# Two-block network on one core: the attention probabilities' 16-bit halves turned by a DMA transpose, one per head, instead of by TensorE

## The reference

```python
G = NUM_HEADS // NUM_KV_HEADS
q = jnp.einsum('bth,oh->bto', x, Wq).reshape(B, T, NUM_HEADS, HEAD_DIM).transpose(0, 2, 1, 3)
k = jnp.einsum('bth,oh->bto', x, Wk).reshape(B, T, NUM_KV_HEADS, HEAD_DIM).transpose(0, 2, 1, 3)
v = jnp.einsum('bth,oh->bto', x, Wv).reshape(B, T, NUM_KV_HEADS, HEAD_DIM).transpose(0, 2, 1, 3)
q = q * cos + _rotate_half(q) * sin
k = k * cos + _rotate_half(k) * sin
qg = q.reshape(B, NUM_KV_HEADS, G, T, HEAD_DIM)
scores = jnp.einsum('bkgtd,bksd->bkgts', qg, k) * scale
scores = jnp.where(causal, scores, -jnp.inf)
attn = jax.nn.softmax(scores, axis=-1)
out = jnp.einsum('bkgts,bksd->bkgtd', attn, v)
return jnp.einsum('bto,ho->bth', out, Wo)
```

## Time and profile before

| | |
|---|---|
| median of 3 runs | 2485.41 us |
| the profiled execution | 2484.75 us, span 2482.8 us |
| busy share of the span | PE 96%, PEld 55%, DVE 72%, ACT 64%, POOL 50% |
| mean granted TensorE clock | 0.986 of full speed |
| DMA, mean share of 16 engines | 27% for the kernel's own queue |
| the attention | about 1597 to 2345 us from the start |
| one pass over eight heads in it | 88.20 us |

### The profile page before, as it was taken

How to read it: one execution, slowest core, us unless ns; L and a number is a source line. 1 busy time by engine, 2 the same in 40 slices (tenths; PEclk the granted TensorE clock), 3 DMA queues, 4 the chain that set the end, 5 groups by cost and what they waited for, 6 DMA issues and landing times. The chain is left out here.

```text
span 2482.8 us, 48888 instructions
## 1 busy us (share of the span) xinstructions
PE 2378.8 (96%) x15424; PEld 1368.9 (55%) x15624; DVE 1787.9 (72%) x3234; ACT 1591.7 (64%) x3327; POOL 1232.0 (50%) x986
## 2 busy tenths in 40 slices
PE   6999999999999999999999998879999999999797
PEld 3555555555555555555555555445555555555443
DVE  6777777777777777777777776577777777788522
ACT  7676776776776776776776775265665656656422
POOL 4455555555555556556556459344434343454223
PEclk8999999999999999999999999999999999999999
DMA  7343343343343343343343341230110110100000
GB/s 248 108 129 111 108 128 111 108 133 105 113 132 107 110 133 109 106 137 109 102 140 109 119 151 56 103 124 1 43 43 1 44 44 1 43 18 1 1 0 34
DMA packets 113827, 218.79 MB, mean 88 GB/s; under 512 B 9632, under 2 KB 43040, under 8 KB 111360
## 3 DMA queue, kind: packets, MB, share of 16 engines
q1 hardware_dynamic: 113536, 215.28, 26.6%
HBM read 212.10 MB, written 3.15 MB: 87 GB/s over the span
## 5 line engine op out<-in xcount | busy, mean ns | idle before, releaser
L256 DVE SCALAR_TENSOR_TENSOR xc<-bank,taps,xc 128x511 f32<-128x511 f32 (+2 forms) x384 | 284.7, 742 | 44.6 <-ACT xc L243 27.4
L984 ACT ACTIVATE E<-wq,cst 128x128 f32<-128x128 f32 x1024 | 311.8, 390 | 2.2 <-PEq L298 2.2
L1268 POOL TENSOR_TENSOR xw<-xt,wdec 128x384 f32<-128x384 f32 x128 | 106.4, 832 | 327.3 <-DVE xt L1119 163.7
L1277 POOL TENSOR_TENSOR acc<-acc,sq 128x512 f32<-128x512 f32 x112 | 172.0, 1536 | 186.8 <-ACT sq L996 186.8
L1911 POOL TENSOR_TENSOR qT<-qT,qrot 128x512 f32<-128x512 f32 x64 | 81.3, 1270 | 368.6 <-DVE qrot L1801 368.6
L1161 DVE SCALAR_TENSOR_TENSOR u<-xc,D,bank 128x512 f32<-128x512 f32 x128 | 95.6, 747 | 210.3 <-PE bank L813 198.8
L1100 DVE TENSOR_TENSOR E<-E,cbm 128x1024 f32<-128x1024 f32 x128 | 242.9, 1898 | 0.8
L61 PE MATMUL bank<-xhi,wx 128*128 128x512 f16 x640 | 242.5, 379 | 0.0
L60 PE MATMUL bank<-xlo,wx 128*128 128x512 f16 x640 | 242.5, 379 | 0.0
L59 PE MATMUL bank<-xhi,wx 128*128 128x512 f16 x640 | 242.5, 379 | 0.0
L1263 POOL TENSOR_TENSOR ecs<-ecs,xcC 128x768 f32<-128x768 f32 x128 | 234.1, 1829 | 0.4 <-POOLq L298 0.4
(11 more groups left out here) (237 smaller groups left out, 6299.4 us busy)
## 6 DMA issues: line engine op xcount, KB each, us to landing
wq<-cs_rows SPq DMA_DIRECT2D x128, 512.0 KB, 4.1
ecs<-ecs_rows SPq DMA_DIRECT2D x128, 384.0 KB, 3.6
wx<-in_w_xbc SPq DMA_DIRECT2D x80, 256.0 KB, 2.7
wz<-in_w_z SPq DMA_DIRECT2D x64, 256.0 KB, 2.7
wo<-in_w_o SPq DMA_DIRECT2D x64, 256.0 KB, 4.0
wq<-in_wq SPq DMA_DIRECT2D x8, 1024.0 KB, 5.7
awo<-in_wo SPq DMA_DIRECT2D x8, 1024.0 KB, 5.0
wkv<-in_wkv SPq DMA_DIRECT2D x8, 512.0 KB, 3.7
```

Of the source, the lines that this page charges most:

```text
L256: self.nc.vector.scalar_tensor_tensor(out=dst[:, d:T], in0=self.k.bank[bank][:, 0:T - d], scalar=self.taps[:, bass.ds(g, 1), b, j, 3 - d:4 ...
L984: ins = nc.scalar.activation(E[t.i % 4][:, h, c], sc.csr[t.i % 2][:, h, c * P:(c + 1) * P], ACT.Relu, scale=-1.0, bias=head(sc.cst, t, c, h))
L1277: nc.gpsimd.tensor_tensor(acc[t.b][:], acc[t.b][:], sq[:], ALU.add).then_inc(acc_done, 1)
```

## The change

- The probabilities are split into halves before they are turned. ACT writes the scaled leading half (`leading_p`) and DVE the rest (`rest_of_p`, now four scalar_tensor_tensor, each reading the fp32 probabilities in SBUF, a scalar per partition, and the leading half in SBUF) into one buffer `phalves` of 20 blocks, ordered so that row block i's rest blocks lie at 5i to 6i and its leading blocks at i + 1, i + 6, and so on.
- SP issues one DMA transpose a head (`turn`) from `phalves` into one of two buffers `pturned`, 20 blocks of 128 x 128 of 16 bits (640 KB). It waits for `rest_of_p` of that head and for `attend` of two heads before. `leading_p` of the next head waits for the transpose to land, `attend` waits for it too, and `exps` waits for `rest_of_p` of the head before, since `probs` is one buffer now.
- PE's ten transposes a head, ACT's three copies and their banks are gone. The projections use four banks in turn (0, 1, 5, 6) in place of two.
- ACT takes the value's leading half from the PSUM bank, and DVE its rest half from the bank (after ACT), where DVE had copied and POOL had subtracted.
- The SwiGLU weights are loaded one piece a head, behind that head's transpose, and the per-column scale `dscale` at the start of the SwiGLU.

```diff
@@ in attention: buffers
-        pr = [sb(f"probs{i}", [P, 1280]) for i in range(2)]
+        pr = sb("probs", [P, 1280])
-        pthi, ptlo = sb("pthi", [P, 1280], F16), sb("ptlo", [P, 1280], F16)
+        ph = sb("phalves", [P, P_BLOCKS * P], F16)
+        pt = [sb(f"pturned{i}", [P, P_BLOCKS, P], F16) for i in range(2)]
@@ SP
+                def turn(n, h):
+                    sp.wait_ge(p_lo, n + 1)
+                    sp.sem_inc(step, 1)
+                    if not (isinstance(n, int) and n < 2):
+                        sp.wait_ge(pv_ready, n - 1)
+                        sp.sem_inc(step, 1)
+                    sp.dma_start_transpose(out=pt[h % 2][:], in_=ph[:]).then_inc(pt_in, 16)
...
+                            if later(g, b, h, 1):
+                                turn(n + 1, h + 1)
+                            if isinstance(g, int) and g < 2:
+                                load_swiglu(k, io, sp, n)
@@ PE
-                            turn(n, h, [0], None)
-                            turn(n, h, [1], None)
...
-                                pe.wait_ge(proj_free, ahead - 1)
+                                ring_free(pe, ahead)
...
-                            turn(n, h, [2, 3], 3 * n + 1)
...
+                    pe.wait_ge(pt_in, 16 * n + 16)
                     for j in range(CH):
...
+                                     (pt[h % 2][:, 6 * j + 1:5 * j + 5], pt[h % 2][:, 6 * j:16 + j:5]), j == 0, j == CH - 1)
@@ ACT
+                def leading_p(n, h):
                     act.wait_ge(exp_done, n + 1)
                     act.wait_ge(rsum_done, n + 1)
+
+                    wait(act, pt_in, 16 * n)
                     for i in range(CH):
+                        nc.scalar.activation(leading_blocks(i), probs(i), ACT.Copy,
+                                             scale=rsum[h % 2][:, i:i + 1]).then_inc(p_hi, 1)
...
-                def leading_v(u, b):
-                    act.wait_ge(v_ok, u + 1)
-                    nc.scalar.copy(vhi[b][:], v[:]).then_inc(kv_hi, 1)
+                def leading_v(u, b, ahead, bank):
+                    act.wait_ge(proj_ready, ahead + 1)
+                    nc.scalar.copy(vhi[b][:], bank[:, :].rearrange("p (t d) -> p t d", d=P)).then_inc(kv_hi, 1)
@@ DVE
-                        nc.vector.tensor_copy(v[:], k.bank[bank][:, :].rearrange("p (t d) -> p t d", d=P)).then_inc(v_ok, 1)
-                        dve.wait_ge(v_ok, u + 1)
+                        dve.wait_ge(kv_hi, 2 * u + 2)
+                        nc.vector.tensor_tensor(vlo[b][:], bank[:, :].rearrange("p (t d) -> p t d", d=P), vhi[b][:],
+                                                ALU.subtract).then_inc(v_lo, 1)
...
-                def rest_of_p(n, u):
-                    bank, at, size = EVAC[u]
-                    dve.wait_ge(pt_hi, 3 * n + u + 1)
-                    nc.vector.tensor_tensor(ptlo[:, at:at + size], k.bank[bank][:, 0:size], pthi[:, at:at + size],
-                                            ALU.subtract).then_inc(pt_lo, 1)
+                def rest_of_p(n, h):
+                    for i in range(CH):
+                        dve.wait_ge(p_hi, 4 * n + i + 1)
+                        out = ph[:, 5 * i * P:(6 * i + 1) * P].rearrange("p (b t) -> p b t", t=P)
+                        ins = nc.vector.scalar_tensor_tensor(out=out, in0=probs(i), scalar=rsum[h % 2][:, i:i + 1],
+                                                             in1=leading_blocks(i), op0=ALU.mult, op1=ALU.subtract)
+                    ins.then_inc(p_lo, 1)
@@ POOL
-                                rest_of_v(g * NB + b + 1, 1 - b)
```

More of the change, by code:

```diff
@@ L1572, in ring, with ring_free @@
                 ahead -= QH
-            return (g * NB + b) * 10 + (PRO + ahead), (PRO + ahead) % 2
+            return (g * NB + b) * 10 + (PRO + ahead), k.bank[RING[(b * 10 + PRO + ahead) % 4]]
+        def ring_free(pe, ahead):
+            wait(pe, proj_free, ahead - 3)
         LAST_OUT = (NG * NB - 1) * 10 + (PRO - QH) + 5
@@ L1662, in output @@
                         w = wo[s][:, h]
-                        mm = product(nc, k.bank[bank][:, :], (ohi[b][:, h, x], olo[b][:, h, x]), (lead(w), rest(w)),
+                        mm = product(nc, bank[:, :], (ohi[b][:, h, x], olo[b][:, h, x]), (lead(w), rest(w)),
                                      h == 0, h == QH - 1)
@@ L1767, in body @@
                             n = item(g, b, h)
-                            for u, (bank, at, size) in enumerate(EVAC):
-                                if u == 2 and later(g, b, h, 1):
-                                    normalise(n + 1, h + 1)
-                                act.wait_ge(pt_ready, 3 * n + u + 1)
-                                nc.scalar.copy(pthi[:, at:at + size], k.bank[bank][:, 0:size]).then_inc(pt_hi, 1)
+                            if later(g, b, h, 1):
+                                leading_p(n + 1, h + 1)
                             if later(g, b, h, 3):
@@ L1871, in body @@
                                 scales(n + 1, h + 1)
-                            for u in range(2):
-                                rest_of_p(n, u)
                             for i, (kind, what) in enumerate(uses):
@@ L1878, in body @@
                                     serve(kind, ahead, bank, n + 3, 0, what[1], what[2])
-                                elif kind != "o":
+                            if later(g, b, h, 1):
+                                rest_of_p(n + 1, h + 1)
+                            for i, (kind, what) in enumerate(uses):
+                                ahead, bank = ring(g, b, h, i)
+                                if kind in "kv":
                                     serve(kind, ahead, bank, 0, g * NB + b + 1, what[1], 0)
-                            rest_of_p(n, 2)
                             if later(g, b, h, 2):
@@ L2220, in program @@
             k.di = k.sb("di", [P, IT, HS], I32, early)
-            k.gs, k.us, k.dscale = (k.sb(n, [P, m], F32, early) for n, m in (("gs", IT), ("us", IT), ("dscale", HS)))
+            k.gs, k.us = (k.sb(n, [P, IT], F32, early) for n in ("gs", "us"))
             k.ffn_in = k.sem("ffn_in")
```

159 lines of the change are left out of this document (75 added, 84 removed).

## The result

The changed kernel takes 2637.67 us in the median of 4 runs (2633.57 to 2639.35), where the kernel before, run beside it, took 2486.03 (2484.25 to 2489.18). The ratio is 1.0606, with a 95% interval of 1.0588 to 1.0624: 6% slower, 152 us. The forecast was 2645.

A forecast was written before the change was run, and what follows sets the result against it. PE was taken to bound the kernel at 9.75 us a head, the DVE-ACT loop close under it at 9.12. POOL's holds on the new rests add 160 us to 2484.75: 2645 us, range 2540 to 2770 (forecast's own 2600 to 2710).

The forecast's parts named there:

- The loop without the collision: DVE-ACT loop of a plain head, from scales to scales, with the new rests but no POOL hold: 9.48 us.
- No collision: Rival: the new rests don't meet POOL at all, so the kernel gets faster, 2476 us; chance 0.07.
- The collision: DVE's rests wait for POOL instructions reading SBUF: 1.05 behind the addition, 1.65 the split, 0.9 the query's rest.
- The estimate with a full block: The same three POOL holds on DVE's rests if the port lock is exclusive: 4.2 us, a head 13.7.
- The sum: Whole kernel: seven groups +145, last group some +15, first four heads +3, less 3 for overlapping edges: +160 us.
- The h = 1 head: Head also projecting key and value: the value's rest waits for ACT's leading half, 16.0 us against 14.85.
- the estimate of 26 us: Transpose of 20 blocks in a row at the skill's 1.31 us a block; a head of 29, 3600 us in all.
- Up to 8 us it costs nothing: DMA transpose, taken as 4.0 us, is hidden up to 8 us; above that 1 us a head for each.
- PE's clock: Idle PE may run at a lower clock: nothing taken, at most 1 us a head (+64) for the range.
- two signs: Expected in the changed profile: PE waits 4 us a head ahead of scores; its busy share falls to two thirds.
- DVE keeps its turn: Rival: the four rests run through once started, only POOL's addition is paid, +59, 2544 us; chance 0.13.
- a slow transpose: Rival: from 8 us on the DMA transpose sets the pace; at 14.8 us, 2906 us in all; chance 0.19.

The follow-up runs named there:

- e_psum: Changed kernel with projections on two banks again and the four rests reading their first input from PSUM bank 5, not the SBUF probabilities: 2466.98 us, ratio 0.9921.
- e_hold_v_n: Changed kernel with POOL's rotation addition waiting for the four rests, ACT taking the value's leading half first, and negated maxima on ACT: 2462.15 us, ratio 0.9894.
- e_vfirst: Changed kernel with ACT taking the value's leading half before the key's, and the two waits that count them exchanged: 2603.02 us, ratio 1.0459.
- e_split: Changed kernel with POOL's weight split of a head put ahead of the rotation sum instead of behind it: 2587.33 us, ratio 1.0404.
- e_copy: Changed kernel with each head's DMA transpose replaced by a plain DMA copy of the same 640 KB: 2631.04 us, ratio 1.0577.
- e_hold_v_n_twice: e_hold_v_n with each head's transpose done twice, the second after the first has landed: 2628.8 us, ratio 1.0572.

## Why the prediction was right, step by step

- **The loop without the collision** was 9.48 us; e_psum, which has no collision, shows 9.32 (1868.20 to 1877.52, starts of `scales`). The terms: `scales` to rotation 0.29 and not 0.47 (1819.52 to 1819.81; the 0.47 of the earlier trace rows runs to the old rests, not to a rotation), rotation 2.28, rests 1.94 against 1.9, mask to next `scales` 4.82 from the rows (2.61 + 2.21) and 4.82 measured (1827.47 to 1832.29). "No collision" was to give 2476, and e_psum gives 2467.
- **The collision** was the step that decided, and it holds term by term. First rest, behind the addition: 1.34 against 0.35 alone, +0.99 (charged 1.05). Second, behind the split: 2.11 against 0.48, +1.63 (1.65). Third, behind the query's rest: 1.51 against 0.65, +0.86 (0.9). Together 3.5 against 3.6. The durations alone are from the groups by shape of e_hold_v_n (busy us, mean ns):

```profile
L1855 DVE SCALAR_TENSOR_TENSOR phalves<-probs,rsum,phalves 128x384 f16<-128x384 f32 x57 | 37.0, 648 | 0.0
...
L1855 DVE SCALAR_TENSOR_TENSOR phalves<-probs,rsum,phalves 128x256 f16<-128x256 f32 x57 | 27.3, 479 | 0.4
...
L1855 DVE SCALAR_TENSOR_TENSOR phalves<-probs,rsum,phalves 128x128 f16<-128x128 f32 x57 | 20.0, 351 | 12.1 <-ACT phalves L1756 6.2 <-DVE qrot L1812 5.9
```

  It was read off two places of the setup and the scan, where other instructions met. The estimate with a full block, 4.2 us, is too much: 3.5 were lost.
- **The heads**: with a split 12.77 (13.1 forecast), without 11.17 (11.4), h = 1 15.8 (16.0); eight 106.66 (108.9). Each is 0.2 to 0.3 high, by `scales` and 0.1 of hold.
- **The sum** has wrong terms that partly cancel, so its nearness is in part luck. From one start of `scales` to that of eight heads later, the two profiled executions differ by 18.3 to 19.6 us in each of the first six groups, 112 us in all where the forecast has 124: that is the error of the heads above. The first heads, forecast at 3 us more, show nothing extra (18.3 in their group). The seventh group costs 24.2, not 20.7: the conversions of SwiGLU weights don't stand in place of the splits there but behind them, so POOL has a fourth instruction and all four rests are held, 6.88 us in place of 5.46:

```profile
2305.86 6.88 DVE L1855 SCALAR_TENSOR_TENSOR phalves<-probs,rsum,phalves 128x128 f16<-128x128 f32 x4 [0.15 <-DVE qrot L1810]
```
```profile
2308.90 1.93 POOL L2008 CAST gi<-gi 128x1376 bf16<-128x1376 int32 x1
```

  The last group gives 14.6 us for the 15 forecast, 2 us lie outside the heads, and the 3 us taken off for edges were not there. Together 153 us between the two profiled executions (2636.2 and 2482.8), and 2645 is 7 us high.
- **The h = 1 head**: `vlo` waits for ACT as said, 2.61 us, and e_vfirst shows it is that wait.
- **The transpose** was 4.0 by estimate and is 4.9; the estimate of 26 us is far off. It is hidden either way. "Up to 8 us it costs nothing" was too generous in one way: the first rest starts late from about 7 us on. What decides is what the delay meets: a split head can lose nothing even at 9.8 (12.77 again), because the hold goes as the rests move, and an h = 1 head loses 2 to 4.
- **PE's clock**: 0.92 in the eight heads. PE fills waits first, and the head's 12.77 us are DVE's and ACT's own durations, which the clock doesn't enter. I took nothing for it, and nothing was needed. In the head from 1819.52 PE's first 3 us after a wait went at 0.53 of the clock (a window in the order of the first one above), and then it waits 2.71 us ahead of `scores`:

```profile
1819.60:1822.60 3.00, 2.97 (x12) 1.58 (x13) 2.75 (x6) 1.92 (x4) 0.58 (x1) 0.53 0.00 0
```
```profile
1832.40 0.38 PE L59 MATMUL bank<-khi,qhi 128*128 128x512 f16 x1 [2.71 <-ACT probs L1743]
```

  So two signs came out smaller than forecast: PE waits 4.34, 2.71 and 2.30 us ahead of `scores` in three heads in a row there and not over 4 in each, and its busy share is 81% (86.67 of 106.66) and not two thirds. The forecast also misread 0.67 in the earlier trace rows: the figure is a mean over time, so two thirds of those 5 us were at 1.2 GHz, not half. Nothing was built on it.
- **DVE keeps its turn** (0.13) is refuted by the 5.46 us and by e_split, **no collision** (0.07) by the same rows, **a slow transpose** (0.19) by the landing and e_copy.

What the change takes from PE stays unused, since the loop through DVE and ACT was only 0.6 us a head behind it. With the collision and the order of the value mended, 24 us of the 70 show (2485.8 to 2462.2, run side by side), with PE busy for 2320 us against 2379 before. In the changed kernel itself PE's busy time hasn't even fallen (2378 us): it does less work at a lower clock.

## What to carry to other kernels

Before moving elementwise work, look at what the other engine of the DVE and POOL pair does at that very moment and whether both inputs will lie in SBUF: the instruction that read one of them from PSUM was free of it here, and moving one engine's work by a wait or by order was worth more (130 us) than the work removed from PE (70). Charge such a meeting one POOL instruction, less some 0.3 us, for each instruction of DVE, whatever their sizes. And check what the shifted engine meets at its new place: here the hold moved on to a four-column instruction, for 0.8 us.

## What the runs showed of the hardware

- DVE and POOL alternate by instruction, and it was one-sided: in a head DVE lost 3.5 us, while POOL's three instructions took 0.2 longer in all. A split that takes 1.90 us alone took up to 2.36 (2.34 in e_split).
- A `tensor_scalar` of 128 x 4 fp32, one tile in SBUF in and one out, is held by POOL like the large ones: 0.17 us alone, 0.97 beside a split.
- The DMA transpose of 20 blocks of 128 x 128 of 16 bits takes 4.9 us from issue to landing, a plain copy of the same 640 KB 3.5. Two in a row took 9.8 (e_hold_v_n_twice). It holds SP's queue for 3.07 us where the plain issues behind it hold it 0.4 to 0.6:

```profile
1827.71 3.05 SPq L1609 DMA_TRANSPOSE pturned<-phalves  x1
1830.81 0.58 SPq L1994 DMA_DIRECT2D gs<-in_gate_s  x1
1831.44 0.42 SPq L1995 DMA_DIRECT2D gs<-in_gate_s_last  x1
```
